# Token normalization of the attention stage: statistics gathered in one period, and its three full-width operations issued by VectorE instead of GpSimd

## The reference

```python
x = L0_attn_x                       # (8, 512, 128)
xn = _layernorm(x, axis=-1)         # (x - mean) / sqrt(var + 1e-5)
x = x + _L0_attn_ref(xn, ...) + _L0_ffn_ref(xn, ...)
# _L0_attn_ref: 16 heads of 64; q, k to unit length, softmax(q.k * scale) v, @ w_out + b_out
# _L0_ffn_ref: 6 times: attention in windows of 32 with rotary tables, then a gated feed-forward
```

## Time and profile before

| | |
|---|---|
| time, median of 3 runs | 4228.49 us (4228.07 to 4228.89) |
| the profiled execution | time 4228.07 us, span of its instructions 4226.3 us |
| busy over the span | PE 3943.4 us (93%), DVE 3877.6 (92%), POOL 2692.1 (64%), ACT 2604.9 (62%) |
| granted TensorE clock, mean | 0.991 of full speed |
| attention stage | to about 965 us; the layers fill the rest |

### The profile page before, as it was taken

The page is one execution under the profiler, slowest core; times in us unless marked ns, Lnnn a source line. Parts: engine busy times, 40 slices in busy tenths (PEclk is TensorE's granted clock), DMA queues, the critical chain, the costliest instruction groups (busy, mean ns, idle before and its releaser), DMA issues. The chain is left out here.

```text
span 4226.3 us, 124870 instructions
## 1 busy us (share of the span) xinstructions
PE 3943.4 (93%) x48616; PEld 2737.1 (65%) x48616; DVE 3877.6 (92%) x4836; ACT 2604.9 (62%) x3780; POOL 2692.1 (64%) x4716
## 2 busy tenths in 40 slices
PE   7999999997999999999999999999999999999996
PEld 4666666665666666666666666666666666666664
DVE  5888888887899999999999999999999999999994
ACT  4666666653566666666666665666666666666663
POOL 5565556545667676676667666666676666666663
PEclk9999999999999999999999999999999999999999
DMA  5454554540000001000110001100011000010000
GB/s 136 93 100 94 98 98 93 103 98 20 24 17 15 20 29 29 17 15 17 31 29 16 16 16 30 29 18 15 16 30 29 20 15 16 20 38 20 15 16 14
DMA packets 342441, 165.08 MB, mean 39 GB/s; under 512 B 114241, under 2 KB 337473, under 8 KB 341185
## 3 DMA queue, kind: packets, MB, share of 16 engines
q1 hardware_dynamic: 342208, 161.99, 17.3%
HBM read 115.67 MB, written 33.69 MB: 35 GB/s over the span
## 5 line engine op out<-in xcount | busy, mean ns | idle before, releaser
L630 POOL TENSOR_TENSOR pn<-es,rden 128x1024 f32<-128x1024 f32 x192 | 366.3, 1908 | 695.3 <-DVE rden L959 695.3
L726 ACT ACTIVATE y<-ps 128x1024 f32<-128x1024 f32 x384 | 372.2, 1021 | 511.1 <-PE ps L1205 511.1
L634 POOL TENSOR_TENSOR t<-t 128x1024 f32<-128x1024 f32 x192 | 454.5, 2367 | 79.8 <-DVE t L911 79.8
L911 DVE TENSOR_TENSOR t<-ps,tabl 128x512 f32<-128x512 f32 x768 | 491.0, 681 | 0.0
L678 ACT ACTIVATE t<-ps,amx 128x512 f32<-128x512 f32 x512 | 347.5, 688 | 224.6 <-DVE amx L815 224.6
L909 DVE TENSOR_TENSOR t<-ps,tabl 128x1024 f32<-128x1024 f32 x384 | 467.2, 1217 | 8.0 <-ACT sq L749 4.3
L636 POOL TENSOR_TENSOR t<-t 128x1024 f32<-128x1024 f32 x192 | 452.8, 2358 | 4.4 <-DVE t L911 4.4
L1013 DVE TENSOR_TENSOR qn<-t,rn 128x2048 f32<-128x2048 f32 x192 | 438.1, 2282 | 5.6 <-POOL rn L399 5.6
L969 DVE TENSOR_REDUCE ss<-sq 128x32 f32<-128x2048 f32 x192 | 437.0, 2276 | 0.0
L1054 PEld LDWEIGHTS ps<-cst,qn 128*128 128x128 f32 x3072 | 350.2, 141 | 118.6 <-issue 61.7
L815 DVE TENSOR_REDUCE amx<-ps 128x2 f32<-128x1024 f32 x256 | 310.9, 1214 | 109.9 <-PE ps L1076 109.6
(11 more groups left out here) (134 smaller groups left out, 8224.5 us busy)
## 6 DMA issues: line engine op xcount, KB each, us to landing
wm<-values_dram SPq DMA_DIRECT2D x128, 256.0 KB, 5.1
y<-values_dram SPq DMA_DIRECT2D x128, 256.0 KB, 4.9
values_dram<-qT SPq DMA_DIRECT2D x64, 256.0 KB, 2.3
tokens_dram<-x SPq DMA_DIRECT2D x96, 128.0 KB
xs<-tokens_dram SPq DMA_DIRECT2D x192, 64.0 KB, 1.8
xw<-tokens_dram SPq DMA_DIRECT2D x192, 64.0 KB, 1.8
xsh<-x SPq DMA_DIRECT2D x48, 128.0 KB
xsh<-x SPq DMA_DIRECT2D x48, 127.0 KB
```

Source lines behind the costliest of these rows:

```text
L630: nc.gpsimd.tensor_tensor(heads(pn[:], H), heads(es[:], H), rden[:].unsqueeze(2).to_broadcast([P, H, KEYS]), ALU.mult).then_inc(l_p, 1)
L634: nc.gpsimd.tensor_tensor(t1[:, 0:INNER], t1[:, 0:INNER], t2[:, 0:INNER], ALU.add).then_inc(l_rotq, 1)
L726: return act.activation(y[:].rearrange("p h (w q) -> p w h q", w=NW)[:, 2 * half:2 * half + 2], src.rearrange("p (w h q) -> p w h q", w=2, ...
L911: sine = nc.vector.tensor_tensor(t23[:, :, lo:lo + DH // 2], q3[:, :, hi:hi + DH // 2], tabl[:, 1, u, i, lo:lo + DH // 2].unsqueeze(1).to_ ...
```

## The change

The statistics of the next batch's tokens (all four blocks) and their moments go together into period 2, ahead of `smallest(i, 3)`; the guess follows at the end of period 2. GpSimd's `newton` on the tokens' root moves from period 3 to the end of period 2. The three operations of `normalize_tokens` leave GpSimd and go to VectorE in period 4, ahead of `smallest(i, 3)`. ScalarE's wait for `s_zero` moves from turn (-1, 2) to a place ahead of all turns.

```diff
 # GpSimd
-            def token_root(b):
-                pool.wait_ge(a_xg, b + 1)
-                newton(pool, a_xr, b, frn[:], fhalf[:], frt[:])
-            def normalize_tokens(b):
-                tokens = acc[:, bass.ds(b * SEQ, SEQ)]
...
-                nc.gpsimd.tensor_tensor(heads(xnn, NU), heads(tokens, NU), ..., ALU.subtract).then_inc(a_dev, 1)
...
-                nc.gpsimd.tensor_tensor(heads(xnn, NU), heads(xnn, NU), frn..., ALU.mult).then_inc(a_xn, 1)
-                nc.gpsimd.tensor_tensor(heads(tokens, NU), heads(tokens, NU), boutb..., ALU.add).then_inc(a_b, 1)
...
-                    if a == 3 and not last:
-                        token_root(b + 1)
-                    if a == 4 and not last:
-                        normalize_tokens(b + 1)
+                    if a == 2 and not last:
+                        pool.wait_ge(a_xg, b + 2)
+                        newton(pool, a_xr, b + 1, frn[:], fhalf[:], frt[:])
 # ScalarE
-                    if s.turn_of(-1, 2):
-                        act.wait_ge(s_zero, 2)
...
+            act.wait_ge(s_zero, 2)
             layers(act, turn)
 # VectorE
+            def normalize_tokens(b):
+                tokens = acc[:, bass.ds(b * SEQ, SEQ)]
+                dve.wait_ge(a_xcp, at("a_xcp", b))
+                past(dve, a_xt, b)
+                nc.vector.tensor_tensor(heads(xnn, NU), heads(tokens, NU), ..., ALU.subtract).then_inc(a_dev, 1)
+                dve.wait_ge(a_dev, b + 1)
+                dve.wait_ge(a_xr, (b + 1) * RS_POOL)
+                nc.vector.tensor_tensor(heads(xnn, NU), heads(xnn, NU), frn..., ALU.mult).then_inc(a_xn, 1)
+                nc.vector.tensor_tensor(heads(tokens, NU), heads(tokens, NU), boutb..., ALU.add).then_inc(a_b, 1)
...
-                    if a in (0, 1) and not last:
-                        token_statistics(b + 1, (2 * a, 2 * a + 1))
-                    if a == 2 and not last:
-                        token_moments(b + 1)
-                    if a == 3 and not last:
-                        token_guess(b + 1)
...
                     if has(0):
                         smallest(i, 2)
                         transpose_weights(a, i, 1)
+                    if a == 4 and not last:
+                        normalize_tokens(b + 1)
+                    if a == 2 and not last:
+                        token_statistics(b + 1)
                     if has(0):
                         smallest(i, 3)
                         transpose_weights(a, i, 2)
+                    if a == 2 and not last:
+                        token_guess(b + 1)
```

More of the change, by code:

```diff
@@ L608, in attend @@
                                                 arn[:].unsqueeze(2).to_broadcast([P, NU * 4, DH]), ALU.mult).then_inc(a_kn, 1)
-                    if a == 3 and not last:
-                        token_root(b + 1)
-                    if a == 4 and not last:
-                        normalize_tokens(b + 1)
+                    if a == 2 and not last:
+                        pool.wait_ge(a_xg, b + 2)
+                        newton(pool, a_xr, b + 1, frn[:], fhalf[:], frt[:])
                     if a == 5 and not last:
                         copy_batch(b + 1)
-            token_root(0)
-            pool.wait_ge(s_ld, 16 * 3)
-            normalize_tokens(0)
+            pool.wait_ge(a_xg, 1)
+            newton(pool, a_xr, 0, frn[:], fhalf[:], frt[:])
             copy_batch(0)
@@ L787, in _, with token_statistics @@
         def _(dve):
-            def token_statistics(b, blocks):
-                for u in blocks:
+            def token_statistics(b):
+                if isinstance(b, int):
+                    dve.wait_ge(s_x0, 16)
+                for u in range(NU):
                     stat = nc.vector.bn_stats(st[:, u], acc[:, bass.ds(b * SEQ + u * P, P)])
                 stat.then_inc(a_st, 1)
-            def token_moments(b):
-                dve.wait_ge(a_st, (b + 1) * 2)
-                past(dve, a_dev, b)
+                dve.wait_ge(a_st, b + 1)
                 nc.vector.memset(gap[:], 0.0)
@@ L805, in token_guess @@
                 dve.wait_ge(a_mv, b + 1)
-                past(dve, a_xn, b)
                 nc.vector.tensor_scalar(fhalf[:], agg[:, :, 1], EPS, 0.5, ALU.add, ALU.mult).then_inc(a_hv, 1)
@@ L810, in token_guess @@
                                         ALU.mult, ALU.add).then_inc(a_xg, 1)
+            def normalize_tokens(b):
+                tokens = acc[:, bass.ds(b * SEQ, SEQ)]
+                dve.wait_ge(a_xcp, at("a_xcp", b))
+                past(dve, a_xt, b)
+                nc.vector.tensor_tensor(heads(xnn, NU), heads(tokens, NU), agg[:, :, 0:1].to_broadcast([P, NU, DIM]),
+                                        ALU.subtract).then_inc(a_dev, 1)
+                dve.wait_ge(a_dev, b + 1)
+                dve.wait_ge(a_xr, (b + 1) * RS_POOL)
+                nc.vector.tensor_tensor(heads(xnn, NU), heads(xnn, NU), frn[:].unsqueeze(2).to_broadcast([P, NU, DIM]),
+                                        ALU.mult).then_inc(a_xn, 1)
+                nc.vector.tensor_tensor(heads(tokens, NU), heads(tokens, NU), boutb[:].unsqueeze(1).to_broadcast([P, NU, DIM]),
+                                        ALU.add).then_inc(a_b, 1)
             def smallest(n, j):
@@ L874, in attend @@
                         transpose_weights(a, i, 2)
[L876 to L879, removed]
+                    if a == 2 and not last:
+                        token_guess(b + 1)
+            token_statistics(0)
             token_guess(0)
             dve.wait_ge(s_ld, 16 * 3)
+            normalize_tokens(0)
             nc.vector.tensor_scalar(sc[:], sc[:], MAX_LOG_SCALE, None, ALU.min).then_inc(s_sc, 1)
```

## The result

The changed kernel takes 4268.17 us (median of 4, 4267.11 to 4270.26), the kernel before 4228.28 (4 runs, 4223.43 to 4228.89): ratio 1.0098, 95% interval 1.008 to 1.0115. It is slower by 40 us. The forecast was 4264, in a range of 4251 to 4282. The profiled execution has a span of 4266.1 us, 39.8 more than the one of before.

The account below looks back on a forecast made before the run. The prediction took a ring through VectorE and PE to bound the attention stage. 4228.07 + 10.5 (statistics) + 16.1 (three operations) + 9.3 (passage) - 0.4 (start) = 4263.6, so 4264 us, range 4251 to 4282.

Parts of the forecast that it names:

- The ring: Attention stage: VectorE 10.04 us up to L833's end, then PE 4.14 until scores release VectorE, set the 14.18 us period.
- the idle place: VectorE's 1.72 us between reciprocals L840 and smallest(i, 1), said to hold all its idle time; work there costs nothing.
- PE sets the period: Rival for the attention stage, chance 0.08: VectorE's insertions cost nothing, L590's lateness returns 11 us; 4226, not slower.
- The statistics: Period 2, statistics and guess inside the ring ahead of L833: 1.5 us for each of seven batches, 10.5 us.
- The three operations: Period 4, normalize_tokens on VectorE inside the ring: 2.3 us for each of seven batches, 16.1 us.
- the 0.3 us for GpSimd's disturbance: Period 4: extra VectorE time for waiting on GpSimd's newton steps beside the three operations, included in their 2.3 us.
- The clock: Rival, chance 0.18: PE's clock falls behind half or all of 14 stalls, adding 12 to 24 us; 4276 to 4288.
- no fall behind a gap of 2.83 us: Argument against the clock rival: after that gap L1150's four matmuls took 0.66 us, against 1.09 at the cold start.
- GpSimd's side: GpSimd loses its three operations (3.35 us) in period 4; L590, 1.6 us late, was counted as gaining nothing.
- The passage: Entry into the layers: L771 queues behind the zeroing of kpad, plus a cold clock; 9.3 us, bounds 6 and 10.5.
- the cover: Passage: 1.35 us of the 7.65 us shift hidden because GpSimd's L634 waits for the zeroing anyway.
- The start: First batch: VectorE finishes the three operations some 0.8 us earlier; -0.4 us taken, bounds -0.9 and +0.5.

Follow-up runs that it names:

- idle_place: Changed kernel with all token work still on VectorE but right behind the reciprocals (periods 1, 2, 4, 5), s_zero awaited in its old turn: 4231.19 us, ratio 1.0007.
- idle_guess_early: Changed kernel with token work behind the reciprocals: statistics in period 0, moments 1, guess 2, full-width operations 4 and 5; s_zero in its old turn: 4225.87 us, ratio 0.9999.
- ring2_before: Kernel before with transpose_weights(i, 2) moved from ahead of L833 to behind smallest(i+1, 0), and reciprocals and token work ahead of both transposes: 4211.44 us, ratio 0.9968.
- zero_back: Changed kernel with only ScalarE's wait for s_zero put back in turn (-1, 2): 4258.82 us, ratio 1.0073.
- stats_back: Changed kernel with statistics (period 1), moments and guess (period 2) moved behind VectorE's reciprocals, the three operations left in place: 4258.7 us, ratio 1.0071.
- split: Changed kernel with the third operation, the addition of the bias, moved from period 4 to the same place in period 5: 4263.36 us, ratio 1.008.
- ring_after: Changed kernel with transpose_weights(i, 2) moved from ahead of L823 to VectorE's idle place: 4246.47 us, ratio 1.0049.

## Why the prediction was right, point by point

**The ring: right.** The distances grew in the periods 2 and 4 and kept their value in 3, 6, 7, 0 and 1; the idle place stayed at 1.73 us; PE's wait went to 1.80 us in period 2 and 2.34 in period 4. Taking the work out of the ring gave the time back (idle_place, idle_guess_early), and taking other work out of it gained (ring2_before). The rival "PE sets the period" falls with the first of these, but it was close: PE's own bound is only 0.26 us lower.

Two things in the argument for the ring were wrong, though the ring itself was not. The sum 10.04 + 4.14 = 14.18 proved nothing, though the forecast used it against that rival: two adjoining stretches of one timeline always add up to the whole. What spoke for the ring was that PE waited for L833 in every period while VectorE came to L833 without a stop. And VectorE's idle time does not all lie in one place: 0.29 us of the 10.04 are the stop ahead of the sum into `acc` (L858), which waits for PE's L1157. In the middle batches it is 0.25 to 0.74 us in every period. So PE's part of the ring reaches from L1111 to L1157, and VectorE's from L858 to L833. The latter takes 6.69 to 6.72 us in every period of the middle batches before, and period 5 is the longest, 14.62, because its stop is 0.74 instead of 0.26. The change put its work behind L858 and paid in full. A small delay ahead of L858 is free: in period 4 of idle_place 0.20 us of it vanish in that stop. Whether more would fit there was not tried.

**The statistics: 1.5 taken, 1.60 measured.** From the sum into `acc` to L823 period 2 takes 8.23 us instead of 6.72, so the work itself costs 1.51. The other 0.09 is the sum, which PE's L1145 releases that much later than before.

**The three operations: 2.3 taken, 2.12 measured.** The step that failed is the 0.3 us for GpSimd's disturbance. Most of it was paid by GpSimd: VectorE's operations took 0.69 to 0.71 us, and GpSimd's steps beside them lost 0.32 to 0.53 each. The order seems to decide who pays: here VectorE's operations followed each other, and each of GpSimd's steps began while one of them ran. The Trainium skill, "GPSIMD Engine Reference", section "Key points", names the pair, a GpSimd operation and a VectorE one with two SBUF inputs. The trace agrees on that, and shows which of the two lost time here.

**The clock: the rival came in part.** It was given 0.18, at the price of 12 to 24 us for half or all of 14 stalls; the forecast's main case had nothing. It came behind five of the 14, all of them behind period 4's stall, and cost 1.6 us each: 8.0. The argument "no fall behind a gap of 2.83 us" rested on one place in one execution, and that was the step that failed: behind this very gap of the last batch (2.82 or 2.83 us) the clock fell in five of seven traces, after the change and in zero_back, stats_back, idle_place and idle_guess_early, and not before the change and in split. The other half of the argument was misread. I had called PE busy throughout from 90 to 94 us, where the kernel before lost 1.7 us; PE's timeline of the kernel before has a gap right ahead:

```profile
89.39 0.65 PE L1087 MATMUL ps<-kpad,wm 32*64 32x128 f32 x18 [1.76 <-issue]
```

Counted over the second to seventh batches of all kernels here, ahead of the projection: behind a gap of 2.28 to 2.36 us the clock fell 12 times in 18 (5 of 6 after, 5 of 6 in zero_back, 2 of 6 in stats_back), behind one of 1.80 to 1.84 twice in 24 (after, zero_back, split, ring_after), and behind 1.66 to 1.74 or 1.16 to 1.23 never in 12. In split the same work with the stall cut in two loses nothing in period 5 in any middle batch. So the fall goes with the longer stall here, but the length alone does not decide: six of the 18 had none.

**The last batch: nothing taken, 2.3 measured.** The stop of 1.61 us in period 5 and the fall of the clock behind the gap of 2.83 share it. zero_back has the fall and not the stop, and its last batch takes 96.18 us, 0.4 over before; split has the stop (1.62) and not the fall, and takes 97.64, 1.9 over. The stop, of 1.3 to 1.6 us, is in seven of the ten kernels, not before the change nor in zero_back and ring2_before. Why it comes stays open.

**GpSimd's side: zero, right.** The 1.6 us by which L590 was late were nobody's. Period 5 took 14.62 before, and the same in idle_place and idle_guess_early, where GpSimd has no normalization.

**The passage: 9.3 taken, 7.8 measured.** L749 moved by 8.0 us against the zeroing, L1036 by 7.6, as forecast. Two sizes were off. The cold clock cost 5.41 - 3.67 = 1.74 us instead of 3.0, since the clock rose during the eight matmuls (at 1010.7 us; they ran from 1007.25 to 1012.66). And the cover, GpSimd held by the zeroing, was put at 1.35 us, though the forecast's own rows give 972.88 - 971.23 = 1.65. It showed as L971's long wait of 1.81 us before; L959 takes 0.25 now, so 1.56 came back: 7.62 + 1.74 - 1.56 = 7.8. In zero_back the time falls by no less than that, so nothing of it is made up later.

**The start: -0.4 taken, -1.0 measured.** PE's first transposes of the normalized tokens, for the 16.33 of the earlier trace rows:

```profile
15.39 1.08 PE L1052 MATMUL ps<-cst,pn 128*128 128x128 f32 x4 [15.39 <-DVE pn L797]
```

They are 0.94 us earlier, about the full 0.8 of the faster subtraction and multiplication; the price that I set against it did not show. But this place varies by half a microsecond from trace to trace: the first scaling of an output starts at 63.3 to 63.8 us in the three kernels with the old start and at 62.2 to 63.4 in the seven with the new one, 0.7 earlier on average.

That the total came out within 4 us is partly luck: 10.3 us for which the forecast had nothing, the clock's 8.0 and the last batch's 2.3, stood against 1.5 too much for the three operations, 1.5 for the passage, and 3.9 in the start, the first batch, the rest of the stage and the layers. One more thing stays open: why the same gap of 2.35 us has a fall behind it at 470 us and none at 589. No run here separates the two.

## What to carry to other kernels

Look for the ring (the chain of waits that leads from an instruction to itself one period later) before asking which engine is busiest: an engine that is idle for 1.7 us in every period can still pay the full length of whatever is put on the other side of that idle place, and the free place is the one where it waits. To find where the ring passes, look for every stop of every engine in it, the small ones too. A full-width operation that a half-idle engine does in 1.0 to 1.3 us for nothing is cheaper than 0.7 us in the ring. And a wait moved to "ahead of everything" is not tidying: ask what is queued behind it on its engine.

## What the hardware did that was not expected

A VectorE operation on 4 elements a partition waits for a full-width `tensor_tensor` of GpSimd that is already running, to its end: 0.12 us undisturbed (idle_guess_early), 0.81 and 1.82 (stats_back), 1.39 as the median of eight (ring_after). It has one source, not two. The Trainium skill, "VectorE: DVE Perf Modes", section "What auto-detection actually checks", says that an operation with a single source and its destination in SBUF, with outermost dimensions both even or equal, runs in a mode that it calls 2×_2P. The Trainium skill, "GPSIMD Engine Reference", section "Key points", counts VectorE's 2-port modes among those that contend with GpSimd; the rows agree with that, in 4-element operations too. In the other direction GpSimd's 16-element steps went from 0.22 to 0.75 us beside VectorE's two-source operations. In these rows the one that starts second loses most of the time, and an edit that moves no such operation at all can cause it, as ring_after showed with 1.2 us a batch.

The clock fell in the midst of a stage in which PE is busy 94% of the time, behind single gaps of 2.3 us, at a cost of 1.6 us each, and not behind each of them (12 of 18).
